# A two-layer graph network on one core: the second layer's count matrices built during the first layer's edge pass

## The reference

```python
x = x + gat(layernorm(x))        # first layer: attention over edges, 8 heads
x = x + ffn0(layernorm(x))       # 6 experts, top 2
x = x + sage(layernorm(x))       # second layer: mean over neighbours
x = x + ffn1(layernorm(x))       # 16 experts, top 2, a layernorm of its own

# gat
e = leaky_relu(a1[src] + a2[dst]); m = segment_max(e, dst); ex = exp(e - m[dst])
out = segment_sum(ft[src] * (ex / segment_sum(ex, dst)[dst]), dst)      # then elu
# sage
agg = segment_sum(x[src], dst)
out = relu(x @ W_self + (agg / max(deg, 1)) @ W_neigh + b)
```

## Time and profile before

| | |
|---|---|
| three runs, us | 2357.85, 2348.93, 2354.08; median 2354.08 |
| profiled execution: span, us | 2350.5 (no other time is listed for it) |
| busy PE / PEld / DVE / ACT / POOL, us | 1674.7 / 1121.0 / 1397.8 / 472.2 / 1035.9 |
| mean granted clock of TensorE | 0.794 |
| edge pass, us | about 73 to 1124.5 |
| neighbour sum, us | about 1503 to 1899.5 |

### The profile page before, as it was taken

One profiled execution on the slowest core, in us unless ns is written; L12 is line 12 of the kernel. 1 busy time (PEld: TensorE's weight loads), 2 busy tenths in 40 slices (PEclk: granted clock), 3 DMA queues, 4 the chain that ended last, 5 costly groups with the idle time before them and its releaser, 6 DMA issues. The chain is left out here.

```text
span 2350.5 us, 34313 instructions
## 1 busy us (share of the span) xinstructions
PE 1674.7 (71%) x8967; PEld 1121.0 (48%) x8967; DVE 1397.8 (59%) x4277; ACT 472.2 (20%) x1077; POOL 1035.9 (44%) x1088
## 2 busy tenths in 40 slices
PE   4466666666667666666337993799999965599970
PEld 3222222222222222222226882599999964488860
DVE  6466666666666666667555115698888845211118
ACT  2100000000000000000322432533333312122222
POOL 1577777777777777773272332000000016222221
PEclk9677776776776767767558996899999976799985
DMA  7455555555555555553325863499000022566644
GB/s 203 108 145 145 142 145 138 144 142 142 145 144 144 145 145 145 145 144 92 99 97 153 246 211 130 103 246 244 2 0 0 0 48 83 160 214 215 214 140 160
DMA packets 255967, 321.42 MB, mean 137 GB/s; under 512 B 64440, under 2 KB 207522, under 8 KB 255767
## 3 DMA queue, kind: packets, MB, share of 16 engines
q1 hardware_dynamic: 198464, 174.84, 27.0%
q0 software_dynamic: 50208, 138.59, 21.6%
q10 hardware_dynamic: 7238, 7.39, 1.1%
HBM read 217.43 MB, written 103.68 MB: 137 GB/s over the span
## 5 line engine op out<-in xcount | busy, mean ns | idle before, releaser
L520 POOL DMA_INDIRECT f_buf<-ftab,scol x806 | 766.2, 951 | 288.5 <-issue 245.3
L920 PE MATMUL ps<-nb_parts,g_counts 128*120 128x256 bf16 x2550 | 305.9, 273 | 0.0
L603 PE MATMUL ps<-ident,f_left 128*128 128x512 f32 x204 | 189.5, 1084 | 135.5 <-ACT f_left L664 135.5
L920 PEld LDWEIGHTS ps<-nb_parts,g_counts 128*120 128x120 bf16 x2550 | 282.8, 133 | 1.9
L612 PE MATMUL ps<-f_diag,f_ones 128*128 128x512 f32 x204 | 186.7, 1070 | 88.6 <-DVE f_diag L754 88.6
L790 DVE TENSOR_TENSOR f_buf<-f_buf,ps 128x1024 f32<-128x1024 f32 x204 | 235.4, 1217 | 17.7 <-ACT ps L673 17.7
L1015 DVE TENSOR_SCALAR g_cell_hot<-nb_table,g_now 128x250 bf16<-128x250 int16 x816 | 231.9, 284 | 0.1
L1014 DVE TENSOR_SCALAR g_src_hot<-nb_table,g_now 128x128 bf16<-128x128 int16 x816 | 203.6, 249 | 27.8 <-PE ps L911 27.5
L751 DVE TENSOR_REDUCE ps<-ps 128x8 f32<-128x1024 f32 x51 | 62.9, 1233 | 250.0 <-PE ps L606 250.0
L1194 POOL MEMSET y_r_half<- 128x25 f32 x1 | 0.1, 120 | 415.1 <-POOLq L874 415.1
L952 ACT CAST g_counts<-ps 128x500 bf16<-128x500 f32 x204 | 115.0, 580 | 222.4 <-PE ps L911 221.3
(11 more groups left out here) (466 smaller groups left out, 2549.4 us busy)
## 6 DMA issues: line engine op xcount, KB each, us to landing
y_wts<-in_L_ffn_w_dram SPq DMA_DIRECT2D x68, 512.0 KB, 4.0
xs<-zero_rows SPq DMA_DIRECT2D x33, 1032.0 KB, 15.0
x_wts<-in_L_ffn_expert_w_dram SPq DMA_DIRECT2D x84, 256.0 KB, 3.2
xs<-zero_rows SPq DMA_DIRECT2D x51, 403.1 KB, 5.0
f_buf<-ftab,scol POOLq DMA_INDIRECT x806
y_xr<-xs SPq DMA_DIRECT2D x34, 258.0 KB, 3.8
x_xr<-xs SPq DMA_DIRECT2D x28, 258.0 KB, 3.1
f_st<-state SPq DMA_DIRECT2D x51, 132.5 KB, 2.3
```

What stands on the lines that cost most here:

```text
L520: nc.gpsimd.indirect_dma_start(out=buf[u][:, j, :], out_offset=None, in_=s.ftab, in_offset=bass.IndirectOffsetOnAxis(ap=s.scol[:, b * CB + ...
L603: nc.tensor.matmul(wide[:, w:w + 4, :], left[b.side][:].rearrange("p j h -> p (j h)"), bc(s.ident[:], 1, 4), start=True, stop=False)
L920: last = nc.tensor.matmul(acc[b.side], counts[b.side][:, t, :], s.parts[:, t, n, :], start=t == 0 and n == 0, stop=t == NT - 1 and n == PA ...
```

## The change

The count matrices depend on the edges alone, so they are built in the edge pass, batch by batch, and stored in DRAM.

- In `stage_flash`, for each batch VectorE builds `cell_hot` in four operations of 128x1000 (`cell_hots`), ScalarE builds `src_hot` as 1 - |iota - row|, clipped at zero, in two halves of eight chunks (`row_hots`), TensorE multiplies them in four quarters (`count`), ScalarE lays the counts out (`lay`), and SP stores 512 KB to `counts` (`keep_counts`).
- To make room in PSUM, the chunk maxima are spread and folded in another way. `wide2` shares the banks of `wide`. The left terms are transposed (eight matmuls of 128 columns) and masked by `nrow` (eight bf16 matmuls) instead of two fp32 and two bf16 matmuls of 512 columns. `cmask`, `diag` and the matmul of `slot_rows` go; `nrow` and `hot_w` are formed from chunk rows that SP now fetches eight times repeated, to 128 partitions. The fold has eight fp32 matmuls of 128 columns with the maxima, broadcast, as the weights.
- In `stage_dense`, counts are loaded in ten blocks of 3, 6 or 3 batches (the first at the end of `blend`). The parts are stationary (128 columns) and the counts move (240 or 480 columns), 150 matmuls a block. The result lies in PSUM by group, so no fold is needed; VectorE adds each of the 408 groups to `accT` by itself, at an offset loaded for it.
- `table_parts` shrinks to `turn_parts`; its other work, ten operations over 816 columns, goes to the end of `stage_open`.

```diff
-GC, GB = 2, 12
-DB = GC * GB
+GC = 2
+GB = CB // GC
+BLOCK, OPENER = 6, 3
+CUT = [0, *range(OPENER, NBT - BLOCK, BLOCK), NBT - BLOCK, NBT - BLOCK // 2, NBT]
+BLOCKS = [(lo, hi) for lo, hi in zip(CUT, CUT[1:]) if lo < hi]
...
@@ stage_flash, SP
+            def keep_counts(b):
+                to = s.counts[b.i:b.i + 1] if isinstance(b.i, int) else s.counts[bass.ds(b.i, 1)]
+                sp.dma_start(to.rearrange("b p c -> p (b c)"), stage[b.side][:].rearrange("p t w -> p (t w)")).then_inc(counts_out[b.side], 16)
...
                     keep_state(b, at_b)
                     if nxt:
                         fetch_state(nxt, at_nxt)
+                    keep_counts(b)
                     clear_slots(b)
...
@@ stage_flash, TensorE
-                pe.wait_ge(diag_ready, b.count(1))
-                for w in range(0, W8, 4):
-                    nc.tensor.matmul(wide[:, w:w + 4, :], left[b.side][:].rearrange("p j h -> p (j h)"), bc(s.ident[:], 1, 4), start=True, stop=False)
-                pe.wait_ge(cmask_ready, b.count())
-                for w in range(0, W8, 4):
-                    last = nc.tensor.matmul(wide[:, w:w + 4, :], nrows16[:], cmask[b.side][:, w:w + 4, :], start=False, stop=True)
+                pe.wait_ge(mx_ready, b.count(1))
+                for w in range(W8):
+                    nc.tensor.matmul(wide[:, w, :], left[b.side][:].rearrange("p j h -> p (j h)"), s.ident[:], start=w % 4 == 0, stop=False, is_transpose=True)
+                pe.wait_ge(near_ready, b.count())
+                for w in range(W8):
+                    last = nc.tensor.matmul(wide[:, w, :], emask[:, w].rearrange("p j h -> p (j h)"), nrow[b.side][:], start=False, stop=w % 4 == 3)
                 last.then_inc(spread, 1)
+
+            def count(b, k):
+                pe.wait_ge(row_ready, b.quarter(k))
+                pe.wait_ge(hot_ready, b.quarter(k))
+                pe.wait_ge(laid, b.quarter(k - 2))
+                for j in range(k * UC, (k + 1) * UC):
+                    last = nc.tensor.matmul(cells[k % 2][:, j % UC // GC, :], src_hot[:, j, :], cell_hot[:, j, :], start=j % GC == 0, stop=j % GC == GC - 1)
+                last.then_inc(built, 1)
...
                     bring(b)
+                    count(b, 0)
+                    look_up(b)
+                    count(b, 1)
                     if nxt:
                         spread_chunks(nxt)
-                    look_up(b)
-                    if nxt:
                         fold_chunks(nxt)
+                    count(b, 2)
+                    count(b, 3)
                     sum_up(b)
                     place_sums(b)
...
@@ stage_flash, ScalarE
+            def row_hots(b, half):
+                n = CB // 2
+                act.wait_ge(built, b.quarter(2 * half + 1 - UNITS))
+                for j in range(n):
+                    nc.scalar.activation(rows_to[:, j, :], s.iota[:], ACT.Abs, bias=now_row[b.side][:, half * n + j:half * n + j + 1])
+                act.drain()
+                nc.scalar.activation(src_hot[:, half * n:(half + 1) * n, :], rows_to[:], ACT.Relu, scale=-1.0, bias=one[:]).then_inc(row_ready, UNITS // 2)
+                act.drain()
+
+            def lay(b, k):
+                if k == 0:
+                    act.wait_ge(counts_out[b.side], b.by_side())
+                act.wait_ge(built, b.quarter(k))
+                o = stage[b.side][:, :, 2 * k * W10:2 * (k + 1) * W10].rearrange("p t (g w) -> p g t w", g=2)
+                nc.scalar.copy(o, cells[k % 2].rearrange("p g (t w) -> p g t w", w=W10)).then_inc(laid, 1)
...
                 def step(b, nxt, after, later):
+                    lay(b, 0)
+                    lay(b, 1)
                     if nxt:
+                        bring_rows(nxt)
+                        row_hots(nxt, 0)
                         copy_left(nxt)
                     weigh(b)
+                    lay(b, 2)
+                    lay(b, 3)
                     if nxt:
+                        row_hots(nxt, 1)
                         fade(nxt)
                     keep_sums(b)
...
@@ stage_flash, VectorE
+            def cell_hots(b, k):
+                dve.wait_ge(built, b.quarter(k - UNITS))
+                at = b.i * CB + k * UC
+                now = s.hots[:, 0, at:at + UC] if isinstance(at, int) else s.hots[:, 0, bass.ds(at, UC)]
+                nc.vector.tensor_tensor(cell_hot[:, k * UC:(k + 1) * UC, :], bc(numbers, 1, UC), bc(now, 2, CELLS), ALU.is_equal).then_inc(hot_ready, 1)
...
                 def step(b, nxt, after, later):
+                    cell_hots(b, 0)
                     spread_tops(b)
                     if nxt:
                         mask_batch(nxt)
+                    cell_hots(b, 1)
+                    if nxt:
                         chunk_tops(nxt)
                     arguments(b)
+                    cell_hots(b, 2)
+                    cell_hots(b, 3)
                     messages(b)
                     if nxt:
                         batch_tops(nxt)
...
@@ stage_dense
+            def multiply(m):
+                lo, hi = BLOCKS[m]
+                if m:
+                    pe.wait_ge(arrived[m % 2], 16 * ((m + 1) // 2))
+                if m >= 2:
+                    pe.wait_ge(added, m - 1)
                 for c in range(2):
+                    for t in range(NT):
+                        for n in range(PARTS):
+                            last = nc.tensor.matmul(sums[m % 2][c][:, 0:(hi - lo) * SLOTS].rearrange("p (b w) -> p b w", w=SLOTS),
+                                                    s.parts[:, t, n, c * 128:(c + 1) * 128], block_of(m)[:, 0:hi - lo, t * SLOTS:(t + 1) * SLOTS],
+                                                    start=t == 0 and n == 0, stop=t == NT - 1 and n == PARTS - 1)
+                last.then_inc(summed, 1)
...
+            def add_groups(first, n, frm):
+                for g in range(n):
+                    at = dve.value_load(s.gbase[0:1, first + g:first + g + 1] if isinstance(first, int) else s.gbase[0:1, bass.ds(first + g, 1)], min_val=0, max_val=N)
+                    w = s.accT[:, :, bass.ds(at, W10)]
+                    nc.vector.tensor_tensor(w, w, frm[:, :, g * W10:(g + 1) * W10], ALU.add)
+                    dve.drain()
...
+            for m in range(len(BLOCKS)):
+                lo, hi = BLOCKS[m]
+                dve.wait_ge(summed, m + 1)
+                add_groups(lo * GB, (hi - lo) * GB, ps[:, 2 * (m % 2):2 * (m % 2) + 2, :])
+                dve.sem_inc(added, 1)
```

More of the change, by code:

```diff
@@ L87 @@
 NPS = 27 * 128
[L88 to L91 removed]
+GC = 2
+GB = CB // GC
+NGR = NC // GC
 UNITS = GB // 2
@@ L594, in _ @@
                 sp.wait_ge(s.slots_out, q * (16 * NBT) + 16 * NBT)
+                for p in range(2):
+                    n = 16 * len(range(p, NBT, 2))
+                    sp.wait_ge(counts_out[p], q * n + (n + 16))
                 sp.sem_inc(kept, 1)
@@ L607, in spread_chunks @@
[L607 to L612, removed]
-                pe.wait_ge(masks_ready, b.count())
-                for h in range(0, HEADS, 4):
-                    last = nc.tensor.matmul(wide2[:, h:h + 4, :], s.nident[:], bc(bmask[b.side][:].rearrange("p j w -> p (j w)"), 1, 4), start=False, stop=True)
+                pe.wait_ge(mx_ready, b.count(1))
@@ new lines, in fold_chunks @@
+            def fold_chunks(b):
+                pe.wait_ge(mx_ready, b.count())
+                pe.wait_ge(masks_ready, b.count())
+                for w in range(0, W8, 4):
+                    nc.tensor.matmul(wide2[:, w:w + 4, :].rearrange("p w (j h) -> p w j h", h=HEADS), s.nident[:], bc(bmask[b.side][:, w:w + 4, :], 3, HEADS), start=True, stop=False)
+                for w in range(W8):
+                    last = nc.tensor.matmul(wide2[:, w, :], mx[b.side][:, w:w + 1].broadcast_to([128, 128]), s.ident[:], start=False, stop=w % 4 == 3)
@@ L959, in _ @@
-            with act.Fori(0, rounds2(act)) as q:
-                def step(b, on):
-                    for k in range(UNITS):
-                        if on[0]:
-                            lay(b, k)
-                    if on[1]:
-                        take(b.back(1))
-                by_rank(act, q, 1, step)
+            for m in range(1, len(BLOCKS)):
+                lo, hi = BLOCKS[m]
+                if m >= 3:
+                    act.wait_ge(summed, m - 1)
+                act.dma_start(loaded[m % 2][:, 0:hi - lo, :], s.counts[lo:hi].rearrange("b p c -> p b c")).then_inc(arrived[m % 2], 16)
@@ new lines, in _ @@
+            for m in range(len(BLOCKS)):
+                lo, hi = BLOCKS[m]
+                dve.wait_ge(summed, m + 1)
+                add_groups(lo * GB, (hi - lo) * GB, ps[:, 2 * (m % 2):2 * (m % 2) + 2, :])
+                dve.sem_inc(added, 1)
+            with dve.Fori(1, rounds2(dve)) as q:
+                late_turn()
+                with dve.Fori(0, NBT) as i:
+                    for row in range(2):
```

(8 more changed lines are left out.)

395 lines of the change are left out of this document (135 added, 260 removed).

## The result

The changed kernel takes 4199.02 us (median of 4 runs, 4196.03 to 4201.09), the kernel before 2354.53 us (4 runs): the ratio is 1.785, with a 95% interval of 1.781 to 1.788. The forecast of slower holds; the time, 2715 us, does not, nor does its range up to 2850. The profiled execution has a span of 4198.1 us, 1847.6 more than before.

A forecast was written before the change was run, and what follows sets the result against it. GpSimd's gathers were taken to bound the edge pass and TensorE the neighbour sum. Span 2350.5 + 305 (edge pass) + 56 (neighbour sum) = 2711.5, and 3.6 from span to median gave 2715 us; range 2530 to 2850.

The forecast's parts named there:

- Edge pass, +305: First layer's edge pass: batches go from 20.05 to 26 us, 298 us over 50, and some 8 at the ends.
- step 6: Edge pass: TensorE spreads the next batch's chunks at the low clock, 3.4 us, done at T + 12.9.
- step 2: Edge pass: TensorE's second count, four matmuls of 250 columns, taken as 0.9 us, done at T + 4.4.
- step 3: Edge pass: ScalarE's second laying out of counts, 0.58 us, and the handover, done at T + 5.0.
- step 5: Edge pass: ScalarE's copy of the next batch's left terms, 0.42 us, late through its queue, done at T + 9.5.
- step 8: Edge pass: VectorE's two masks, 0.5 us, and merge, 0.84, close the circle at T + 26.7, the period.
- step 4: Edge pass: ScalarE's row fetch and first row one-hots, eight Abs at 0.29 us among them, 4.1 us, done at T + 9.1.
- step 7: Edge pass: VectorE, idle since T + 3.5, runs reduction, arguments, two cell_hots, messages and batch_tops, done at T + 25.4.
- Neighbour sum, +56: Second layer's neighbour sum: VectorE's 408 single adds at 1.05 us become the bound, 453 us; bounds -40 to +95.
- The third: Rival with more waits: TensorE at 1.2 GHz throughout, fade behind second row_hots, 29 us a batch; 2820 to 2870 us, chance 0.14.
- TensorE as the bound of the neighbour sum: Rival: edge pass slows, but adds under 0.64 us let TensorE set the neighbour sum; 2540 us, chance 0.07.
- The gathers as the pace: Rival: left-term copy not late, gathers set the edge pass, which grows by 8 us only; 2245 to 2418 us, chance 0.12.

The follow-up runs named there:

- e1: Changed kernel with the three late loops of the neighbour sum put behind a condition (more than one round): 2714.74 us, 1.154 of the kernel before.
- e2: Changed kernel, no condition, its inner late loops cut to 3 batches in place of 51: 2811.43 us (one run).
- e8: Against e1: ScalarE does the eight Abs of the first row one-hots twice a batch: 2831.39 us (one run).
- e6: Against e1: each group's sum is added at a constant place, without a register load, so sums land in wrong places: 2555.09 us (one run).
- e3: Against e1: ScalarE's step copies the next batch's left terms first, ahead of both lays and the first row one-hots: 2406.94 us.

## Why the prediction was right and wrong

**The step that failed is the sum.** It has a term for the edge pass and one for the neighbour sum, and none for the loops from 1 to the number of rounds that stand behind the neighbour sum. I took them as empty and named them nowhere; no rival had them either. They cost 1486 us, 80% of the difference. The trace of before held a hint that I did not read: its loops count from 0 and so had to run, but their only comparison stands behind the body (L933, 1897.0 us). With the bound and the start in the new code, both 1 here, that raises the question which e1 and e2 answer: what does a queue do when it comes to a body that should not run? It could have been priced as well: 16 chunks x 2 one-hots, 16 matmuls of 250 columns, four copies, 150 matmuls and eight adds a batch, in one chain, 51 times.

**The rest of the sum.** With the body skipped the time is 2714.74 us against the forecast 2715, and 1.154 of the kernel before, so slower was right for the reasons given too. That the time fits to 1 us is luck: +32 on the edge pass, -24 on the neighbour sum and -8 elsewhere cancel.

- *Edge pass, +305.* Measured +337.3. The walk holds well up to step 6. Counted from the first `cell_hots` (1386.22), `count(b,1)` ends at 4.75 us (step 2: 4.4), `lay` at 5.4 (step 3: 5.0), `copy_left` at 9.85 (step 5: 9.5), the spread at 12.7 (step 6: 12.9), and the period is 26.46 (step 8: 26.7). Eight Abs take 2.44 us (step 4: 2.3). Behind step 6 two errors nearly cancel: the masks of step 8 begin at 24.6 (step 7: 25.4), but `merge` then waits 0.73 us for TensorE, a wait that the walk doesn't have. VectorE's busy time a batch is 799 / 51 = 15.7 us; my 16.2 was a slip, as 13.5 + 5.1 - 2.8 is 15.8. Two choices behind the walk were off: I took 26 where it had given 26.7, and 20.05 us for a batch of before where its batches were merged every 19.86. 50 x (26.46 - 19.86) is 330, and 7 more lie at the ends.
- *Step 6, the clock.* The level was right: TensorE idles four microseconds in front of the spread and the clock granted is 0.50, the lower level, before it and in it (windows of the changed kernel at an earlier batch). But it is 0.50 from 1012 to 1018 us as well, while TensorE works, so that the pause brings it down isn't shown:

```profile
1018.00:1022.00 4.00, 0.00 (x0) 0.00 (x0) 0.00 (x0) 3.62 (x10) 2.87 (x4) 0.50 0.98 325
1022.00:1024.00 2.00, 1.30 (x6) 1.30 (x7) 0.00 (x0) 0.42 (x1) 1.60 (x2) 0.50 0.80 164
```

- *ScalarE's tables, nothing.* Right: the changed kernel too has one table load in all, of 1283 ns. For the Abs, the Trainium skill ("ScalarE: Activation LUTs", section on what ACT_TABLE_LOAD costs) gave 0.294 us for each that follows another, 2.35 for eight; the trace agrees with it, as eight more of them add 4.78 - 2.44 = 2.34 us in e8.
- *Neighbour sum, +56.* Measured +31.8. TensorE's 264 us were right (265.3 in e6). (The row gave 1.80 / 15 = 0.12 us for a matmul of 256 columns and not my 0.11; but the first block's 150 of 240 columns take 15.54 us, which is 0.11 for 256.) The term that was too large is the add: put at 1.05 us, it takes 0.99 on average, 0.95 for most. I had 0.85 from the load to the add, where the rows have about 0.75 (2090.6 to 2091.35), and I charged part of a drain behind the add, where the drain (0.18) begins with the add and ends with it. The bound below, 0.80, held, and so did the statement that the loads decide: with eight in one the pass loses 106 us, without any 160.
- *Elsewhere.* The first expert stage with `blend` is 5.4 us shorter, where I took 0, at most 5, for the tables that left it; no run tests whether they are the cause, nor why the second expert stage is 2.1 us shorter. The opening hides its new work, as the first gather starts at 74.1 us and before at 74.9.

**The rivals.** None had the extra pass. The third (2820 to 2870 us) also reached past the range that was said to hold it, up to 2850. TensorE as the bound of the neighbour sum needs the loads gone (e6). The gathers as the pace, chance 0.12, needed a detour of at most 2.8 us; e3 shows what decides instead: not the amount of ScalarE's work as such, but that the copy of the left terms stood behind it. The detour was real (VectorE waits 9.3 us at its end), and moving one call cuts the wait to 3.6 us.

## What to carry to other kernels

Ask of every loop with a computed bound how often its body runs when the bound says never, and price that body as if it ran, until a condition ahead of it is seen; the rows of an old loop can show where its comparison stands. When new work is put into an in-order queue, put it behind the operation that another engine is waiting for: the same work cost 6 us a batch ahead of the copy (26.4 against 20.3) and at most 0.5 behind it (20.3 against 19.9). Small operations at computed places are paid by the register steps, not by their elements; load several offsets at once, and count what the steps still cost.

## What the runs showed that I had not expected

- These loops are tested behind their body only: one comparison at 3740.1 us for a body entered at 2263.2, and in the kernel before one at 1897.0 for a body entered at 1503.4.
- One register load of eight values takes 0.60 us, of one value 0.30; eight sets of register steps still cost some 2.8 us.
- The chain of load, steps, add and drain gets longer on average while blocks of counts and zero rows are on the move: 47 adds in 50 us from 1940 (DMA share 1.09), 52 from 2040 (0.16). Single loads take up to 1.01 us, at 1850 to 1860, and at most 0.32 from 2040 to 2090. That the transfers are the cause was not tested, and from 1860 to 1876, at a DMA share of 1.11, the adds stand 0.95 us apart as well.
